# A two-layer network on one core: unread products added at 37 places of TensorE's list

## The reference

```
xn = layernorm(x)
# layer 0: 16 heads of 16; 8 experts, each token takes 2
s = causal_softmax_attention(xn) @ w_out + b_out
f = sum over 2 experts: weight * ((silu(xn @ w1[e]) * (xn @ w2[e])) @ w3[e])
x = x + s * silu(f);  xn = layernorm(x)
# layer 1: 16 key heads of 128, 32 value heads of 128
q, k, v = conv4(xn @ W_qkv.T);  k = k / |k|
for t:  state = state * decay[t] + k[t] (v[t] - k[t] state) * beta[t];  o[t] = q[t] state
s = (rmsnorm(o) * silu(xn @ W_z.T)) @ W_out.T
f = 2 shared experts + 2 of 16 routed experts (gelu)
x = x + s * silu(f)
```

## Time and profile before

| | us |
|---|---|
| median of 3 runs (lowest to highest) | 1293.44 (1292.91 to 1293.97) |
| the profiled execution | 1291.24 |
| its span, first to last instruction | 1288.1 |
| TensorE busy | 1246.8 |
| VectorE busy | 1086.3 |
| ScalarE busy | 912.3 |
| GpSimd busy | 907.4 |
| mean granted clock of TensorE | 0.979 |

### The profile page before, as it was taken

The page is one execution under the profiler, slowest core; times in us unless marked ns, Lnnn a source line. Parts: engine busy times, 40 slices in busy tenths (PEclk is TensorE's granted clock), DMA queues, the critical chain, the costliest instruction groups (busy, mean ns, idle before and its releaser), DMA issues.

```text
span 1288.1 us, 33126 instructions
## 1 busy us (share of the span) xinstructions
PE 1246.8 (97%) x12248; PEld 1066.1 (83%) x12248; DVE 1086.3 (84%) x2385; ACT 912.3 (71%) x2537; POOL 907.4 (70%) x1179
## 2 busy tenths in 40 slices
PE   8999999899999999999999999999999999999996
PEld 7656455678889898989898889899999989989895
DVE  5887466899698998999999888988888879888887
ACT  4001654597878787887878888788787888787784
POOL 4121533757797778758787888887888789887664
PEclk9887999899999999999999999999999999999997
DMA  7921101222110111111111113122212221321221
GB/s 231 250 74 47 36 30 62 82 46 75 23 53 25 41 34 46 27 35 34 59 43 42 31 53 101 42 65 65 71 55 71 66 84 44 84 73 48 74 67 46
DMA packets 59771, 81.66 MB, mean 63 GB/s; under 512 B 6300, under 2 KB 44316, under 8 KB 59612
## 3 DMA queue, kind: packets, MB, share of 16 engines
q1 hardware_dynamic: 54876, 65.26, 18.5%
q0 software_dynamic: 4736, 14.29, 4.0%
HBM read 66.69 MB, written 12.71 MB: 62 GB/s over the span
## 4 chain that ended last, share of the span: by engine, by line
PE 68%; DVE 17%; ACT 7%; issue 4%; POOL 2%; DMA 2%; SPq 0%; POOLq 0%; DVEq 0%; ACTq 0%
PE ps L1112 26%; PE ps L1460 3%; PE ps L1474 3%; PE ps L1444 3%; PE ps L1403 3%; PE ps L1413 3%; PE ps L1416 2%; PE ps L1445 2%; DVE yv L1861 2%; PE ps L1470 2%; DVE ZL L1970 2%; PE ps L1383 2%; PE ps L1174 2%; PE ps L1297 2%; PE ps L1218 2%
## 5 line engine op out<-in xcount | busy, mean ns | idle before, releaser
L2225 ACT ACTIVATE XY<-ps 128x512 f16<-128x512 f32 x384 | 221.1, 602 | 88.4 <-PE ps L1416 86.5
L1970 DVE TENSOR_TENSOR ZL<-ps,cst 128x256 f16<-128x256 f32 x384 | 152.4, 415 | 21.9 <-PE ps L1403 21.0
L1861 DVE SCALAR_TENSOR_TENSOR yv<-ps,cw,yv 128x511 f32<-128x511 f32 (+2 forms) x192 | 142.3, 743 | 9.4 <-ACT yv L2169 6.6
L1112 PE MATMUL ps<-XH,WVh 128*128 128x256 f32 (+1 forms) x384 | 132.8, 346 | 0.5 <-ACT st L2273 0.3
L1112 PE MATMUL ps<-XH,WVl 128*128 128x256 f32 (+1 forms) x384 | 122.7, 319 | 0.0
L1112 PE MATMUL ps<-XL,WVh 128*128 128x256 f32 (+1 forms) x384 | 122.3, 319 | 0.0
L1413 PE MATMUL ps<-ZL,XY 128*128 128x64 f16 x1536 | 104.1, 193 | 0.8 <-DVE ZL L1970 0.4
L1416 PE MATMUL ps<-XY,ZL 128*128 128x64 f16 x1536 | 104.0, 193 | 0.0
L1403 PE MATMUL ps<-XY,LT 128*128 128x64 f16 x1536 | 95.5, 193 | 2.5 <-ACT XY L2225 2.4
L2259 ACT ACTIVATE sq<-O 128x128 bf16<-128x128 f32 x256 | 79.3, 310 | 26.0 <-DVE O L2020 12.0
L1403 PEld LDWEIGHTS ps<-XY,LT 128*128 128x128 f16 x1536 | 77.1, 98 | 19.2 <-issue 9.2
(11 more groups left out here) (329 smaller groups left out, 4355.2 us busy)
## 6 DMA issues: line engine op xcount, KB each, us to landing
RC<-crow SPq DMA_DIRECT2D x128, 128.0 KB
WV<-in_WV SPq DMA_DIRECT2D x16, 512.0 KB, 3.5
exr<-in_ex SPq DMA_DIRECT2D x16, 384.0 KB, 3.2
WK<-in_WK SPq DMA_DIRECT2D x16, 256.0 KB, 2.8
WO<-in_WO SPq DMA_DIRECT2D x16, 256.0 KB, 3.2
rows_out<-st SPq DMA_DIRECT2D x7, 512.0 KB, 4.9
KS<-spread SPq DMA_DIRECT2D x12, 256.0 KB, 8.4
QS<-spread SPq DMA_DIRECT2D x12, 256.0 KB, 12.0
```

Source lines behind the costliest of these rows:

```text
L1112: m = pe.matmul(o, a, b, start=c + k == 0, stop=c == 1 and k == 2)
L1861: m = dve.scalar_tensor_tensor(out=dst[:, k:512], in0=ps[:, bk, 0:512 - k], scalar=cw[:, h, j, 3 - k:4 - k], in1=dst[:, k:512], op0=ALU.mu ...
L1970: leave(dve.tensor_tensor(half(ZL[:, k - 2], k, 0), p, lv(k), ALU.mult), "a", u, k)
L2225: leave(act.activation(changed(u, k), ps[:, bank("b", u, k), :].rearrange("p (c n t) -> p c n t", c=2, t=1 << (k - 1)), ACT.Copy), "b", u, k)
```

## The change

Beside the list the planner now keeps, for each TensorE item, when TensorE came free, when the item starts and when it ends, all in the planner's own estimated time (`AT`). A new function goes through the list once. For each item it adds up an amount of array work for the items that ended in the last `SPAN` before its start (`dense` gives the amount of each label, and the products already added count too). Where less than `DENSE` is there, it adds as many products of 256 columns as are missing, but no more than fit into the idle time ahead of the item, and at least one. `HELD` is empty. `enter` then issues these products into the bank just granted, ahead of the item's own waits: the identity `idh` times the 256 columns of `cb`. The item's own first product overwrites the bank, so nothing reads what they leave. The result is 62 products at 37 items.

```diff
+SPAN, DENSE = 3.4, 3000
+HELD = {}
...
         order, banks = {e: [] for e in idle}, []
+        self.AT.clear()
...
             ready.remove(p)
+            if p.eng == "PE":
+                self.AT[p.label] = idle["PE"], first[2], end
             idle[p.eng] = end
...
+def dense(x):
+
+    what = x[0]
+    if what == "p1":
+        return 96 * (x[3] + 1) + 256
+    if what == "sc":
+        return 100 * (4 - x[3])
+    if what == "pv":
+        return 128 * (4 - x[3])
+    if what in ("exg", "exv", "ck", "cq", "cv", "Zt", "up", "y", "gt"):
+        return 3072
+    return {"exd": 1024, "op": 2048, "ov": 2048, "su": 1536, "sd": 1024, "dn": 1024, "KS": 1024, "U": 512, "so": 1024, "gram": 1024,
+            "r": 1024, "c": 512, "b": 512, "a": 256, "x1": 256, "kn": 512, "Vt": 512, "ot": 512, "ln1": 256, "sT": 1024, "tn": 128,
+            "cnt": 256, "slot": 256, "cum": 1024, "crow": 512}.get(what, 256)
+
+
+def spare_products(at, order):
+
+    spare, past = {}, deque()
+    for x in order["PE"]:
+        ended, start, end = at[x]
+        start += HELD.get(x, 0.0)
+        while past and past[0][0] < start - SPAN:
+            past.popleft()
+        lack = DENSE - sum(n for _, n in past)
+        if start > SPAN and lack > 0 and x[0] not in ("pv", "cum", "crow"):
+            n = min(-(-lack // 256), max(int((start - ended - 0.1) / 0.11), 1))
+            spare[x] = n
+            past.append((start, 256 * n))
+        past.append((end, dense(x)))
+    return spare
...
+SPARE = spare_products(Plan.AT, ORDER1)
...
             def enter(*key):
                 for s, n in room(*key):
                     w.wait_ge(s, n)
+                if key in SPARE:
+                    w.wait_ge(s_c0, 4)
+                for _ in range(SPARE.get(key, 0)):
+                    pe.matmul(ps[:, bank(*key), 0:256].rearrange("p (k t) -> p k t", k=2), idh, cb[:], start=True, stop=True)
                 return bank(*key)
```

More of the change, by code:

```diff
@@ L1 @@
+from collections import deque
 from contextlib import ExitStack
@@ L182 @@
 class Plan:
+    AT = {}
     GRAIN = 0.09700
```

## The result

The changed kernel takes 1297.95 us (median of 11 runs, 1291.51 to 1303.79); the kernel before, run beside it, 1292.49 us (11 runs, 1288.91 to 1295.8). The ratio is 1.0042, interval 1.0027 to 1.0057: 5.4 us slower (3.5 to 7.4), where +3.0 was forecast. The profiled execution took 1298.39 us, its span is 1296.2 us, against 1291.24 and 1288.1 of before.

The account below looks back on a forecast made before the run. TensorE was taken as the bound, busy 1246.8 of 1288.1 us. Terms 3.4 + 0.3 + 2.3 - 0.7 - 0.4 - 1.0 - 0.9 = +3.0 us, put on the median 1293.44, gave 1296.4 us, range 1291.0 to 1300.0.

Parts of the forecast that it names:

- Items 98 to 274: Middle places, 22 products at full clock with no gap to hide in: pure cost, +3.4 us, bounds 2.4 to 5.7.
- change of kind: Middle places: going from 2-byte to 4-byte operands costs 0.08 us at 13 of 19 places, 1.0 us of the +3.4.
- p1's late stretch: Layer 0's row maximum from quad (1, 6) on: clock low again, 11 products at 0.21 us each, +2.3 us.
- p1 up to there: Row-maximum part before the long low stretch: cost +0.3 us, clock gains -0.7 and -0.4 us.
- The halved gain of 1.5 us at 59.28 us: Six expert products at 59.28 us: preventing the second short clock fall gains 1.5 us; half taken, -0.7 us.
- Ahead of (ln1, 4): Second layer's first transpose of the second half: 10 products keep the clock high for the gate product, -1.0 us.
- rival D: The eight transposes of (ln1, 4) to (ln1, 7) lose the held clock before the gate product: 1297.4 us, chance 0.15.
- Ahead of (ot, 63): Last output transpose: 9 products may raise the clock for the last output products, -0.9 us, from -2.5 to +0.3.
- A: The clock holds through p1, VectorE's waits go and p1's products hide: -5.5 us, 1287.9 us, chance 0.10.
- B: Whole kernel: costs and gains meet, middle costs only 2.4 us, tail gets most of its gain: -0.1 us, chance 0.20.
- C: Whole kernel: products with an identity as stationary side do not move the clock, only costs remain: +6.2 us, chance 0.10.

Follow-up runs that it names:

- tripled kernel: Three times the products at the 19 middle places (66), none elsewhere, against the kernel before: 1301.39 against 1295.37 us, ratio 1.0049.
- p1-places run: Only the changed kernel's 21 products up to item 86 stay, against the kernel before: 1292.91 against 1293.73 us, ratio 0.9996.
- the kernel with the two gaps alone: Only the 10 products ahead of (ln1, 4) and 9 ahead of (ot, 63) stay, against the kernel before: 1291.98 against 1293.73 us, ratio 0.9984.
- the fastest kernel: Two products ahead of each p1 step among items 58 to 86, 9 ahead of (ot, 63), against the kernel before: 1287.74 against 1292.0 us, ratio 0.9961.
- the tail alone: Only the 9 products ahead of (ot, 63), against the kernel before: 1294.14 against 1296.25 us, ratio 0.9985.
- p1 places and gaps together: The changed kernel without its 22 middle products, against the kernel before: 1297.59 against 1295.37 us, ratio 1.0005.
- the last of the dense kernels: 110 dense p1 and expert-step products, plus products in the waits around the gate product and in the tail, against before: 1292.3 against 1296.25 us, ratio 0.9967.
- the dense kernel with the two gaps: 110 dense p1 and expert-step products, plus 10 ahead of (ln1, 4) and 9 ahead of (ot, 63), against before: 1293.36 against 1295.37 us, ratio 0.9981.
- the first dense kernel: Two products ahead of each p1 step among items 12 to 37 and 58 to 86, six at (exg, 3, 0), against before: 1290.32 against 1293.73 us, ratio 0.9978.

## Why the prediction was right, and where it was not

It forecast slower by 3.0 us, for the reason that the products lie on TensorE's path while the places that could hold the clock are left bare. The measured +5.4 us is in the range of times, but the +3.0 itself lies below the interval of 3.5 to 7.4. The direction was reasoned; that the sum came as near as it did is in part luck, since terms that were too high and too low by 0.2 to 1.9 us partly cancel. (A small slip of reading: the two short low stretches, from 48.6 and 58.8 us, both stand in the page's second slice.) Point by point:

**Items 98 to 274: right, a third too high.** Taken +3.4 us; 22 x 0.112 = 2.5. In the timeline of PE of after, single products stand between 4-byte work of two sorts:

```profile
140.31 0.28 PE L1141 MATMUL ps<-cb 128*128 128x256 bf16 x1
140.52 0.49 PE L1252 MATMUL ps<-QS,KS 50*128 50x512 f32 x2
...
141.53 0.28 PE L1141 MATMUL ps<-cb 128*128 128x256 bf16 x1
141.57 0.48 PE L1157 MATMUL ps<-XH,exh 128*128 128x512 f32 x1
141.89 0.39 PE L1157 MATMUL ps<-XL,exh 128*128 128x512 f32 x1
```

The step that failed is the 0.08 us of a change of kind, taken from expert products behind p1. That row's 0.07 us belong to that neighbourhood; the tripled kernel shows none of it here.

**p1's late stretch: right, by its mechanism and size.** Taken +2.3 us for 11 products at the low level. From p1 (1, 6, 0) to (exv, 5, 0), ten of them, before takes 11.60 us and after 13.73, the same again in the p1-places run: 0.213 us each. The first steps of quads (1, 6) and (1, 7), with three products between them, in the timeline of PE of after:

```profile
100.18 0.47 PE L1230 MATMUL ps<-KS,QS 48*128 48x128 f32 x2
100.59 0.40 PE L1235 MATMUL ps<-cb 128*128 128x128 bf16 x2
100.78 0.42 PE L1141 MATMUL ps<-cb 128*128 128x256 bf16 x1
...
104.39 0.48 PE L1230 MATMUL ps<-KS,QS 48*128 48x128 f32 x2
```

They are 4.21 us apart, before 3.57; the 4.4 of the forecast was for four products, but the first of the four stands ahead of the row at 100.18. And VectorE, which had to wait 0.26 us for a quad, waits longer, in the timeline of DVE of after:

```profile
108.71 3.32 DVE L1789 TENSOR_REDUCE Mp<-ps 128x2 f32<-128x1024 f32 x4 [0.52 <-PE ps L1235]
...
116.86 0.69 DVE L1767 TENSOR_TENSOR hT<-hT,ps 128x512 f32<-128x512 f32 x1 [3.19 <-PE ps L1157]
```

**p1 up to there: the term that had the wrong sign.** +0.3 - 0.7 - 0.4 = -0.8 us were taken. From (exg, 3, 0) to p1 (1, 6, 0) the four traces with the sparse products take 45.41, 45.76, 45.77 and 46.37 us, the five with none there 43.69 to 45.39 (mean 44.7): +1.1 us, some of it scatter, since three of the five stand at 45.3 to 45.4. (The sum priced six products; seven stand there besides the three at the start, 0.1 us more.) The halved gain of 1.5 us at 59.28 us was read from one execution in which the clock was up for 3.4 us between two short low stretches. Of the eleven traces without dense products there, only before and the tripled middle took 7.2 us from there to (exg, 4, 0); the others took 8.75 to 9.08, whether products were added or not, with one long low stretch over it. What the change was to prevent is mostly a matter of the single run. That error of 1.9 us is the largest of the sum.

**Ahead of (ln1, 4): rival D's outcome.** Taken -1.0 us. The timeline of PE of after:

```profile
244.79 1.25 PE L1141 MATMUL ps<-cb 128*128 128x256 bf16 x10
245.88 0.60 PE L1148 MATMUL ps<-cst,st 128*128 128x128 f32 x4
...
250.17 0.65 PE L1157 MATMUL ps<-XH,wabh 128*80 128x512 f32 x1 [0.87 <-DVE XL L1846]
250.62 0.63 PE L1157 MATMUL ps<-XL,wabh 128*80 128x512 f32 x1
```

The same two gate products in the kernel with the two gaps alone, from the same list of work:

```profile
241.85 0.44 PE L1159 MATMUL ps<-XH,wabh 128*80 128x512 f32 x1 [0.87 <-DVE XL L1848]
242.12 0.40 PE L1159 MATMUL ps<-XL,wabh 128*80 128x512 f32 x1
```

With the ten products the clock stays at 1.00 in the gap and through the transposes, in all five traces that have them. Without, in eight traces, it fell somewhere from 0.15 us ahead of the first of these transposes to 3.0 us behind it, always ahead of the gate product. So the ten do put off the fall. In three of the five it then came at the gate product all the same, 0.04 to 0.42 us behind its start (26.62, 26.62, 26.63 us from (gt, 0) to (gg, 1)), and in two not there (25.07, 25.06). The eight traces without have 25.97 to 27.39, mean 26.3. So the products gain 1.2 us when the fall misses the gate product and lose 0.3 us when it hits it: -0.3 us in the mean of the five, against -1.0. The step that failed is that the high level, once held over the gap, would reach the end of the gate product. D put the fall in front of the gate product; it came at its start, right behind the light work that D named. On the rule that D cites, that the high clock does not engage for transposes (the Trainium skill, "TensorE: Matmul & The Clock Gate", Part 4), these traces are not decisive: a clock that was already up stayed at 1.00 from 245.9 to 250.2 us, through eight transposes and the four of the key, and fell right behind them.

**Ahead of (ot, 63): right, but half of what it is worth.** Taken -0.9 us, with -2.5 as a bound. The timeline of PE of after:

```profile
1282.25 0.63 PE L1527 MATMUL ps<-cst,O 128*128 128x128 f32 x4 [2.85 <-ACT O L2310]
1282.71 1.15 PE L1141 MATMUL ps<-cb 128*128 128x256 bf16 x9
1283.97 0.66 PE L1527 MATMUL ps<-cst,O 128*128 128x128 f32 x4
1285.69 0.39 PE L1157 MATMUL ps<-WOh,OGH 128*128 128x256 f32 x1 [1.07 <-POOL OGL L2342]
```

Here the clock had not fallen; the transposes of (ot, 63) start 1.7 us behind those of (ot, 62), as before, because at the high level the nine fill the wait that was there and no more. In three of six traces with the nine it had fallen, as the prediction took it to have, and the nine took 1.9 us at the low level; yet the clock was up again for both of the last output products. The timeline of PE of the changed kernel's second trace:

```profile
1287.14 2.07 PE L1141 MATMUL ps<-cb 128*128 128x256 bf16 x9
1289.04 0.60 PE L1527 MATMUL ps<-cst,O 128*128 128x128 f32 x4
1290.17 0.39 PE L1157 MATMUL ps<-WOh,OGH 128*128 128x256 f32 x1 [0.52 <-POOL OGL L2342]
```

The tail is 30.9 to 31.4 us long in all these six, 33.0 to 33.6 in six without; that is 2.1 us, or 1.8 if the one trace in which it failed is counted, and the tail alone was timed at -1.9. That trace is of the fastest kernel; the clock fell 0.7 us after the nine had begun and stayed down:

```profile
1274.51 1.46 PE L1144 MATMUL ps<-cb 128*128 128x256 bf16 x9
1275.76 1.11 PE L1530 MATMUL ps<-cst,O 128*128 128x128 f32 x4
1277.49 0.58 PE L1160 MATMUL ps<-WOh,OGH 128*128 128x256 f32 x1 [0.61 <-POOL OGL L2345]
```

The step that was too careful: of the 2.5 us that the clock can give back here 0.9 was taken, and it gave 2.1 in six traces of seven.

**By the measured terms** the sum is 2.5 + 1.1 + 2.5 - 0.3 - 1.8 = +4.0 us (2.5 for late p1 is the whole column to (tn, 1), mean of the four with against the five without), against +3.0 forecast and +5.4 and +5.7 measured.

**The rivals.** A's mechanism is real, and what it promised, -5.5 us, was nearly had (-5.0) by the late p1 dense with the tail: the clock can hold through p1 if the steps of its light stretches all get products (items 58 to 86 in all five traces, items 12 to 37 in one of three), and p1's late part then runs at VectorE's pace. In both traces of the changed kernel it doesn't, and there quad (1, 5) and others stay bare, which was the argument against it. In single runs it may: the changed kernel's fastest run, 1291.51 us, has a mean clock of 0.989, its slowest, 1303.79 us, 0.974. B's -0.1 us lies outside the interval. C is refuted: products with the identity as the stationary side move the clock, from 0.9766 to 0.9896 with 110 of them. Its +6.2 us was nevertheless nearer to both measurements than the forecast, since the forecast's gains came only in part.

**What stays open.** The three parts timed alone give 3.6 - 0.5 - 2.1 = +1.0 us, with some 3 us of uncertainty, the whole +5.4 and +5.7. So some 4.5 us of the change are not in its parts as timed alone, and 1.4 to 1.7 not in the items' sum above. By clock: p1 places and gaps together 0.9823, with the middle added 0.9801 and 0.9779, though the middle by itself changes no clock. That loss of some 0.003, about 2.7 us at the rate above, is at the edge of what these runs tell apart (each mean has about 0.002 to 0.003 to either side). Whether the middle's products move the fall onto the gate product, or this is scatter, no run here decides.

## What to carry to other kernels

Work that nothing reads pays only where TensorE isn't the bound: in a wait, or beside an engine that sets the pace anyway, and there it must cover the whole light stretch, since with bare quads between them the clock fell here all the same and every product cost 0.21 us. Price it by asking which engine waits for TensorE in that stretch and for how long; that wait is all that can be won (in this kernel, 2 x 0.11 us a step hidden beside 3.32 us of VectorE a quad gave -4.0 us, and a clock of 0.995 over the whole kernel gave no more). Where the profile shows a fall, look whether a second trace has it at the same place before putting a gain on preventing it.

## What the runs showed of the hardware

- The granted clock stays low although TensorE is never idle: 23.80 of 23.80 us busy at 0.50 in before, 17.10 of 17.10 in after. The steps there use 48 of the 128 rows. Ahead of the fall there were short waits: TensorE was busy for 5.63 of the 6.2 us ahead of it in before (80.0 to 86.2 us), for 3.10 of 3.4 us in after (96.6 to 100.0). Whether these waits or the thin steps brought the fall is not separated, as the dense kernels removed the waits too: with two full products of 256 columns a step the clock was 1.00 and TensorE busy for 26 of 26 us (84 to 110 us) in each of the five traces that had them.
- In the early stretch the same two products a step did not always do so. In the last of the dense kernels, TensorE fully busy, the clock was low over most of p1's first part (windows); there, and in the dense kernel with the two gaps, TensorE had waited 1.5 and 1.9 us for a DMA just ahead of p1, and in the first dense kernel, with the clock at 1.00, it had not:

```profile
46.60:63.20 16.60, 16.60 (x72) 8.70 (x70) 8.94 (x11) 0.00 (x1) 5.52 (x6) 0.50 1.06 254
```

- A 256-column bf16 product with full stationary side costs 0.110 to 0.112 us at 2.4 GHz between the 4-byte products of the middle, with nothing on top for the change of type, and 0.213 us at 1.2 GHz.
- Behind the ten products the clock stayed at 1.00 through twelve transposes and their waits, 4.3 us; in three traces of five it fell within 0.42 us behind them, and without the ten it fell ahead of them or among them in all eight traces.
- The same weights' DMA, issued at about 37 us, lands at different times: the split that waits for it starts from 48.9 to 53.0 us over the 14 traces, a band of 4 us.
